# A decoder layer with routed experts: register loads of the expert loop taken eight at a time, without run-time bounds checks

## The reference

```
x = x + attn(norm(x))          # windowed attention with quantized weights, 16 heads
x = x + xattn(norm(x), ctx)    # scores against 64 context rows, top 54 kept, softmax
x = x + ffn(norm(x))           # shared expert + 16 routed experts, 4 per token

scores = sigmoid(gate_w @ x) + gate_b
weights, indices = top_k(scores, 4);  weights = weights / weights.sum()
out = silu(x @ w1s) * (x @ w3s) @ w2s
    + sum over the token's 4 experts e of weights[e] * (silu((x @ w1[e]) * (x @ w3[e])) @ w2[e])
```

## Time and profile before

| | |
|---|---|
| time, median of 3 runs | 846.86 us (846.11 to 847.08) |
| the profiled execution | 847.12 us, its span 845.3 us |
| PE busy | 670.7 us (79%) |
| VectorE busy | 639.4 us (76%) |
| POOL busy | 513.2 us (61%) |
| ScalarE busy | 414.0 us (49%) |
| granted TensorE clock, mean | 0.930 |
| expert phase | from about 504 us to the end |

### The profile page before, as it was taken

How to read it: one execution, slowest core, us unless ns; L and a number is a source line. 1 busy time by engine, 2 the same in 40 slices (tenths; PEclk the granted TensorE clock), 3 DMA queues, 4 the chain that set the end, 5 groups by cost and what they waited for, 6 DMA issues and landing times. The chain is left out here.

```text
span 845.3 us, 19054 instructions
## 1 busy us (share of the span) xinstructions
PE 670.7 (79%) x4034; PEld 550.3 (65%) x4034; DVE 639.4 (76%) x2096; ACT 414.0 (49%) x1196; POOL 513.2 (61%) x403
## 2 busy tenths in 40 slices
PE   0766777667536789999986437899999999999994
PEld 0555666566424556665654316799999999998993
DVE  4699999999843577777665775777777777777773
ACT  0543545445113456554552145556666666666662
POOL 0587887877610006555777751577766775877775
PEclk9999989979877899999998778999999999999998
DMA  6811111300002334576334543577787786887774
GB/s 183 289 33 38 50 37 38 124 19 25 19 19 94 119 119 157 204 259 237 138 139 143 193 164 92 100 117 134 127 135 132 120 134 115 140 139 126 131 116 54
DMA packets 77614, 100.45 MB, mean 119 GB/s; under 512 B 10256, under 2 KB 70816, under 8 KB 76960
## 3 DMA queue, kind: packets, MB, share of 16 engines
q0 software_dynamic: 26736, 37.64, 24.8%
q1 hardware_dynamic: 50784, 61.74, 24.8%
HBM read 50.97 MB, written 52.95 MB: 123 GB/s over the span
## 5 line engine op out<-in xcount | busy, mean ns | idle before, releaser
L1480 POOL DMA_INDIRECT out_dram<-yw,xg x143 | 225.0, 1573 | 115.3 <-issue 55.1
L1079 POOL DMA_INDIRECT xs_scratch<-rows,slot x128 | 125.4, 980 | 131.2 <-issue 107.7
L1368 PE MATMUL cbank<-w,stc_hi 112*128 (+1 forms) x572 | 123.5, 309 | 2.9 <-issue 1.4
L1368 PE MATMUL cbank<-w_hi,xtc_hi 128*128 x286 | 105.6, 369 | 5.8 <-DVE xtc_lo L1380 5.6
L1368 PEld LDWEIGHTS cbank<-w,stc_hi 112*128 112x128 f32 (+1 forms) x572 | 88.8, 188 | 30.1 <-issue 23.6
L1380 DVE TENSOR_TENSOR xtc_lo<-cbank,xtc_hi 128x256 fp32r<-128x256 f32 x143 | 60.7, 424 | 46.1 <-ACT xtc_hi L1375 45.6
L1368 PE MATMUL cbank<-w_hi,xtc_lo 128*128 x286 | 92.7, 324 | 0.0
L460 PE MATMUL ps_o<-ident,pv 128*128 128x128 f32 x288 | 48.2, 326 | 55.9 <-ACT ot L296 50.4
L1368 PE MATMUL cbank<-w,xtc_hi 128*128 x286 | 92.5, 323 | 0.0
L1420 ACT ACTIVATE sgc<-hh 128x128 f32<-128x128 f32 x143 | 44.4, 310 | 92.3 <-DVE hh L1414 90.9
L460 PEld LDWEIGHTS ps_o<-ident,pv 128*128 128x128 f32 x288 | 40.0, 168 | 64.8 <-POOL pv L261 44.4
(11 more groups left out here) (214 smaller groups left out, 1766.9 us busy)
## 6 DMA issues: line engine op xcount, KB each, us to landing
xg<-xs_scratch SPq DMA_DIRECT2D x143, 144.0 KB, 2.7
w<-w13r_dram SPq DMA_DIRECT2D x8, 704.0 KB, 6.1
x_in<-x_dram SPq DMA_DIRECT2D x32, 128.0 KB, 2.4
w_hi<-ctx_t_dram SPq DMA_DIRECT2D x8, 512.0 KB, 4.0
x_scratch<-u SPq DMA_DIRECT2D x32, 128.0 KB, 2.2
w_hi<-x_scratch SPq DMA_DIRECT2D x8, 512.0 KB, 4.0
out_dram<-w SPq DMA_DIRECT2D x16, 256.0 KB
w<-w2r_dram SPq DMA_DIRECT2D x4, 1024.0 KB, 9.9
```

Of the source, the lines that this page charges most:

```text
L1079: nc.gpsimd.indirect_dma_start(t["xs"], bass.IndirectOffsetOnAxis(ap=slot[:, n % 2, k:k + 1].bitcast(U32), axis=0), rows[:, n % NROW, k // ...
L1368: last = nc.tensor.matmul(out, stationary, moving, start=j == 0, stop=j == len(pairs) - 1)
L1480: nc.gpsimd.indirect_dma_start(t["out"], bass.IndirectOffsetOnAxis(ap=xg[:, p, ID:ID + 1].bitcast(U32), axis=0), yw[:, p % YB, :], None, c ...
```

## The change

The table is laid out as three rows of 143 numbers, `table[0, k, n]`, so that eight entries of one kind lie side by side. A helper, bulk, loads eight neighbouring entries with one load instruction into eight registers and leaves out the checks. All four queues use it:

- SP loads the starts of tiles n to n + 7 at n = 0, 8, 16, ..., in front of the transfer of tile n.
- PE loads the experts of tiles 0 to 7 in front of tile 0's matmuls, and those of tiles n + 4 to n + 11 in front of the matmuls of h_mm for n = 4, 12, 20, ...
- VectorE does the same with the columns at the beginning of y_ev.
- POOL loads the entries of before for tiles 0 to 7 in front of scatter 0, and those of tiles n + 4 to n + 11 behind scatter n = 4, 12, 20, ...

```
--- before.py
+++ after.py
@@ -552,9 +552,9 @@
         eng.wait_ge(self.s_p, 2)
         link(v.tensor_scalar(self.e[:, :], bank[0:1, N_TILES:2 * N_TILES], float(NE - 1), None, ALU.min))
         link(v.scalar_tensor_tensor(self.start[:, :], number[0:1, :], float(P), bank[0:1, 0:N_TILES], ALU.mult, ALU.add))
-        link(v.tensor_copy(table[:, :, 0], self.start[:, :]))
-        link(v.tensor_copy(table[:, :, 1], self.e[:, :]))
-        link(v.tensor_scalar(table[:, :, 2], self.e[:, :], float(D), None, ALU.add))
+        link(v.tensor_copy(table[:, 0, :], self.start[:, :]))
+        link(v.tensor_copy(table[:, 1, :], self.e[:, :]))
+        link(v.tensor_scalar(table[:, 2, :], self.e[:, :], float(D), None, ALU.add))
         eng.wait_ge(self.s_p, 3)
         link(v.tensor_scalar(before[:, :], side[0:1, 0:N_TILES], 0.0, 1.0, ALU.max, ALU.add))
 
@@ -1344,7 +1344,9 @@
 
         def load(eng, n, p):
 
-            start = eng.value_load(table[0:1, n, 0:1], min_val=0, max_val=N_ROWS - P)
+            if n % BULK == 0:
+                starts[:] = bulk(mybir.EngineType.SP, table[:, 0, :], n, 0, N_ROWS - P)
+            start = starts[n % BULK]
             if n >= AHEAD:
                 landed(eng, n - AHEAD)
             eng.dma_start(xg[:, p, :], t["xs"][bass.ds(start, P), :]).then_inc(s_e[p], 16)
@@ -1379,27 +1381,39 @@
             f["t_hi"].wait(eng, n)
             f["t_ev"].sig(nc.vector.tensor_tensor(xt_lo[:, p % 2, :, :], x_t(p), xt_hi[:, p % 2, :, :].bitcast(F32), ALU.subtract))
 
-        expert_of = {}
-        column_of = {}
-
-        def expert(eng, n):
-            return eng.value_load(table[0:1, n, 1:2], min_val=0, max_val=NE - 1)
-
-        def column(eng, n):
-            return eng.value_load(table[0:1, n, 2:3], min_val=D, max_val=D + NE - 1)
+        def bulk(engine, row, n, low, high):
+
+            _, values = nc.values_load_multi_w_load_instructions(
+                row[0:1, n:min(n + BULK, N_TILES)], engines=[engine], min_val=low, max_val=high,
+                skip_runtime_bounds_check_because="the table is worked out on the chip and clamped to its range there")
+            return values
+
+        starts, expert_of, column_of, others_before = [], {}, {}, {}
+
+        def experts(n):
+            if n < N_TILES:
+                expert_of.update(enumerate(bulk(mybir.EngineType.PE, table[:, 1, :], n, 0, NE - 1), n))
+
+        def others(n):
+            if n < N_TILES:
+                others_before.update(enumerate(bulk(mybir.EngineType.Pool, before[:, :], n, 1, N_TILES + 1), n))
+
+        def columns(n):
+            if n < N_TILES:
+                column_of.update(enumerate(bulk(mybir.EngineType.DVE, table[:, 2, :], n, D, D + NE - 1), n))
 
         def h_mm(eng, n, p):
 
             if n == 0:
-                expert_of[0] = expert(eng, 0)
-            e = expert_of[p]
+                experts(0)
+            if n % BULK == BULK // 2:
+                experts(n + BULK // 2)
+            e = expert_of[n]
             f["t_ev"].wait(eng, n)
             f["hh"].wait(eng, n - 2)
             f["h"].sig(accumulate(R[2 + p % 2][:, 0:2 * HID], [
                 (x[:, p % 2, ch, :], w[:, ch, bass.ds(e, 1), :]) for ch in range(DC)
                 for x, w in ((xt_hi, w13_hi), (xt_hi, w13_lo), (xt_lo, w13_hi))]))
-            if n < N_TILES - 1:
-                expert_of[(p + 1) % U] = expert(eng, n + 1)
 
         def h2_(eng, n, p):
 
@@ -1445,7 +1459,7 @@
 
         def y_mm(eng, n, p):
 
-            e = expert_of.pop(p)
+            e = expert_of.pop(n)
             if n < NE:
                 eng.wait_ge(s_lo, n + 1)
             f["st_ev"].wait(eng, n)
@@ -1458,27 +1472,28 @@
 
         def y_ev(eng, n, p):
 
-            c = column_of.pop(p) if n else column(eng, 0)
+            if n == 0:
+                columns(0)
+            if n % BULK == BULK // 2:
+                columns(n + BULK // 2)
+            c = column_of.pop(n)
             f["y"].wait(eng, n)
             if n >= YB:
                 eng.wait_ge(s_done, n - YB + 2)
             f["y_ev"].sig(nc.vector.tensor_scalar(yw[:, p % YB, :], R[6 + p % 2][:, 0:D], xg[:, p, bass.ds(c, 1)], None,
                                                   ALU.mult))
-            if n < N_TILES - 1:
-                column_of[(p + 1) % U] = column(eng, n + 1)
-
-        others_before = []
 
         def scatter(eng, n, p):
 
             f["y_ev"].wait(eng, n)
-            if n % BULK == 0:
-                _, others_before[:] = nc.values_load_multi_w_load_instructions(
-                    before[0:1, n:min(n + BULK, N_TILES)], engines=[mybir.EngineType.Pool], min_val=1, max_val=N_TILES + 1)
-            eng.wait_ge(s_done, others_before[n % BULK])
+            if n == 0:
+                others(0)
+            eng.wait_ge(s_done, others_before.pop(n))
             settle(eng)
             nc.gpsimd.indirect_dma_start(t["out"], bass.IndirectOffsetOnAxis(ap=xg[:, p, ID:ID + 1].bitcast(U32), axis=0),
                                          yw[:, p % YB, :], None, compute_op=ALU.add).then_inc(f_o[p].sem, 16)
+            if n % BULK == BULK // 2:
+                others(n + BULK // 2)
 
         DEPTH = 8
         plan = [(0, "y", 0, load), (0, "g", 8, scatter),
@@ -1540,7 +1555,7 @@
             t[name + "g"] = t[name][0:TOK, :].rearrange("(g t p) d -> g t p d", t=GT, p=P)
         w13_hi = sb("w13_hi", [P, DC, NE, 2 * HID], R32)
         pre = CrossInputs(sb, sem, w13_hi[:, :, :, :].bitcast(F32).rearrange("p c e h -> p (c e h)"))
-        keep = dict(w13_hi=w13_hi, pre=pre, base=pre.base, table=sb("table", [1, N_TILES, 3], I32),
+        keep = dict(w13_hi=w13_hi, pre=pre, base=pre.base, table=sb("table", [1, 3, N_TILES], I32),
                     before=sb("before", [1, N_TILES], I32), pad_at=sb("pad_at", [1, NE], I32),
                     **{n: sem(n + "_exp") for n in ("s_w", "s_pad_at", "s_hi", "s_lo")})
         attention_phase(nc, dict(t, x1=t["x1"].rearrange("(g p a) d -> g p a d", p=P, a=WIN)), lambda eng: pre.load(eng, t),
```

## The result

The changed kernel takes **868.55 us** (median of 4 runs, 865.9 to 869.35) against 846.87 us (4 runs, 846.11 to 847.08): ratio **1.025, 95% interval 1.023 to 1.028**. It is slower, and far outside the range of the prediction. The profiled execution of the changed kernel took 865.9 us, its span is 863.9.

What follows compares the result with a forecast made beforehand. The prediction took a ring of ScalarE and VectorE, 2.15 us per tile, to bound the expert stage and POOL the end. Gains of 2.9, 3.3 and 0.3, 6.5 us, took 846.86 to 840.4 us, range 837 to 844.6.

Steps and rivals of the forecast that it cites:

- on PE and VectorE I take 0.30 + 0.30 = 0.61 us: Length of a load of eight: a single load's 0.30 us plus about 0.30 for seven more values; ends 0.31 and 1.12.
- the upper end, 1.12 us: Longest load of eight allowed for on PE and VectorE, taken from POOL's longest load.
- the rival on the slower side: VectorE's load ahead of yw costs eight singles, 2.48 us, making xtc_lo 1.9 late 17 times: about 872 us; 5%.
- The 0.1 us to issue yw behind the load: VectorE, 17 tiles: estimated issue time, so yw starts at 607.96, just in time for xtc_lo at 608.44.
- The ring of 2.15 us sets the pace: Expert stage: ScalarE and VectorE wait for each other (hh, sgc, xtc_hi, xtc_lo), 2.15 us per tile; PE just keeps up.
- The PE rival: Expert stage: PE is the bound, so a tile falls from 2.177 to 1.98 us: 818.5 us in all; 4%.
- Late tiles, -2.9: Expert stage: 3.4 us above the ring, mostly late PE loads; 0.5 kept as remaining, gain 2.9.
- GpSimd's end, -3.3: Kernel end: moving POOL's load and dropping checks starts the last scatter 2.7 us earlier; with 0.55 of hh, gain 3.3.
- Start, -0.3: Before the stage: SP's first load without checks brings the row transfer and first h_mm earlier, gain 0.3 us.
- Cost of zero for a load of eight ahead of yw and h_mm: In 17 tiles the load just fits: 0 on VectorE (worst 8.7 us) and 0 on PE (worst 10.4 us).
- The sum: Late tiles 2.9, POOL's end 3.3 and start 0.3 gain 6.5 us off the median 846.86: 840.4 us.
- One sign that I named: Chain of waits would name VectorE and ScalarE instead of PE, with PE idle about 0.17 us per tile.

Runs made afterwards that it cites:

- the old order: The kernel before's plan order: t_mm and t_hi in stage 3, sgc standing between hh and xtc_hi; kernel before 846.87 us, changed kernel 868.55 us.
- the twos: Changed kernel with TensorE and VectorE loading two values behind every second h_mm and yw: 840.17 us, ratio 0.991.
- the new order: t_mm, t_hi one pass earlier, t_hi ahead of sg_ on ScalarE: 822.86 us with single loads without checks, 849.11 in kernel before, 870.31 in changed kernel.
- the loads of eight behind: Changed kernel with TensorE's and VectorE's loads of eight issued behind h_mm and yw of n % 8 == 3, not ahead of the next: 874.42 us, ratio 1.034.

## Why the prediction was wrong

The step that failed is one term: "on PE and VectorE I take 0.30 + 0.30 = 0.61 us". It measured 2.13 and 1.89. The slope per further value, 0.043, was taken from GpSimd's row less SyncE's and carried to two engines for which no row of a load of several values stood. On SyncE it holds (0.04); on GpSimd, whose load of one value no run has, eight cost 0.57 in all. Even the upper end, 1.12 us, came from a slow one of GpSimd's and was no bound for another engine: the trace of before had no upper bound at all, and then the price of eight single loads, 2.4 us, is the end to take. I wrote that number down, as the rival on the slower side, and gave it 5%. The 0.1 us to issue yw behind the load was short too: it takes 0.23 at the median.

That rival has the mechanism and the sign of what happened, but only one of the two places, and 872 against 868.55 is in part luck. It got there by two errors that cancel. It charged VectorE alone 17 x 1.9 us, and each of its loads cost 0.9, because the queue starts the load while the engine still has issued work. And it charged TensorE nothing, where each load cost 0.6. Its price begins too early as well: it charges 0.38 us for each load of 1.0 us, while loads of 0.97 and 1.00 us, behind yw and h_mm, cost nothing in the ring. Ahead of them no load of that length was tried.

The Trainium skill, Runtime: NRT & Kernel Launch, section Instruction fetch mechanics, gives about 200 ns per register even in bulk. TensorE's 0.23 to 0.28 and VectorE's 0.22 to 0.23 come near it here, 10 to 40% above, though these loads are from SBUF; SyncE's 0.04 is far from it. I had set that rule aside for the one row that was of the wrong engine.

The other steps hold, as the versions without the long loads show:

- *The ring of 2.15 us sets the pace.* Shown, though one reading for it was wrong: 2.11 us is the distance of one pair of tiles in the chain and not TensorE's own pace. In the kernel before TensorE starts a tile every 2.15 us (median of the first product of h_mm, 560 to 815 us), as it must in a ring of 2.15. The ring stays at 2.15 in every version with the old order, whatever is taken off TensorE's queue, and breaks to 2.00 with the order. The PE rival's 818.5 is wrong as a result of this change, but its price for a tile, 1.98, was close to the 2.004 measured once the ring was gone.
- *Late tiles, -2.9.* 3.4 us before, 0.1 to 0.3 with single loads without checks. Shown, though it was load and check together.
- *GpSimd's end, -3.3.* From tile 137 to the end 26.3 us before, 23.5 with the loads moved: -2.8. Right in kind.
- *Start, -0.3.* Right by itself, and turned round by the long load. When the stage begins varies from run to run, so I count from SyncE's first table load to the first hh, in the versions with the old order: 7.53 us before; 7.21 to 7.25 with TensorE's loads of one or two and SyncE's of eight (four profiles), -0.3; 7.54 with loads of four; 8.27 to 8.36 with TensorE's load of eight (three profiles, the changed kernel among them), +0.8.
- *Cost of zero for a load of eight ahead of yw and h_mm.* It follows from the 0.61 and falls with it. Whether 0.61 would have cost nothing there is not shown: no run has a short load in that place.
- *The sum.* -6.5 gave 840.4. The change with the single loads put back measures 840.46, the twos 840.17. To a tenth this is luck (late tiles gave 3.1 to 3.3 instead of 2.9, GpSimd's end 2.8 instead of 3.3).

One sign that I named was wrong as well. With the single loads the chain of waits still names TensorE for all of its time, though sgc and xtc_lo wait for each other in 119 of 119 tiles. The chain and the PE column can't see this ring, with or without loads in the queue. The chain from 560 to 800 us of that version:

```profile
by line: PE cbank L1370 79.9%; PE cbank L1359 10.1%; PE cbank L1443 5.1%; PE cbank L1444 5.0%; issue 0.0%
```

## What to carry to other kernels

An instruction's price is a price on one engine. Before a cost is carried from one queue to another, ask for a row of the same engine; without one, the end of the range is the plain multiple of what the trace does show. Batching small operations on a queue saves only the part of the price that doesn't grow with their number, and it can turn many delays that fit into holes into one that fits into none: compare the length of the batch with the cover at one place, not with the sum of the holes. And where removing a delay brings little, look for the second limit just beneath: here the single loads without checks in the new order gave 25 us, without the new order 6, and the new order alone nothing.

## What the runs showed of the hardware

- A register load from SBUF costs 0.30 us on TensorE and VectorE for one value and about 0.25 and 0.22 us for each further one; on SyncE 0.27 and 0.04; on GpSimd 0.57 for eight (these are medians of the kernels before and changed; in the versions with short loads on VectorE, GpSimd's eight took up to 0.78 and SyncE's up to 0.65). On the first two, eight in one instruction (2.13 and 1.89 us) save 0.3 and 0.6 us over eight single ones (2.4 and 2.5).
- The queue of an engine runs ahead of it: in the ring, a register load of four or eight on VectorE started 0.2 to 0.5 us before the instruction ahead of it in program order did, and in the new order, where hh itself had to wait, together with hh. TensorE had about 0.7 us of weight loads (0.9 of products) in hand when its load of eight began, in the new order about 0.95 (1.2). What a load costs is its length less this cover, and less any wait that the next instruction would have had anyway.
- The granted clock fell from 1.00 to 0.5 (1.2 GHz) for 3.5 us twice inside the stage with the loads of eight behind, each time after some 1.9 us without a weight load on TensorE, but idle times as long elsewhere in that run left it at 1.00.
- On TensorE each single load of before had a check of 151 ns and an assertion of 18 ns behind it, in the same queue (on VectorE 190 and 23); these lines are from the kernel before.

```profile
L1386 PEldq FUSED_REGOPS  x143: 151/151/165, 509.4 to 826.9; - x143
L1386 PEldq SEQ_ASSERT  x143: 18/18/28, 509.6 to 827.1; - x143
```
